# GRU scan on TensorE: r's state product of the row scans as two products, with v and with u

## The reference

```python
seq = xs.reshape(b * A, T, c) @ Wi.T + bi            # 192 -> 64
x_gates = seq @ W_ih.T + b_ih
def step(h, xg):
    hg = h @ W_hh.T + b_hh
    xr, xz, xn = split(xg); hr, hz, hn = split(hg)
    r = sigmoid(xr + hr)
    z = sigmoid(xz + hz)
    n = tanh(xn + r * hn)
    h_new = (1.0 - z) * n + z * h
out = hs @ Wo.T + bo
x = x + (right + down + left + up) / 4.0
```

## Time and profile before

| | |
|---|---|
| median of three runs | 2478.38 us |
| profiled execution | 2490.38 us |
| its span, first to last instruction | 2488.6 us |
| TensorE clock granted, mean | 0.985 of full speed |
| busy: PE matmul, PEld weight load | 2186.1 us (88%), 1416.7 us (57%) |
| busy: DVE, ACT, POOL | 2014.4 (81%), 1579.7 (63%), 1532.9 us (62%) |

### The profile page before, as it was taken

One profiled execution on the slowest core, in us unless ns is written; L12 is line 12 of the kernel. 1 busy time (PEld: TensorE's weight loads), 2 busy tenths in 40 slices (PEclk: granted clock), 3 DMA queues, 4 the chain that ended last, 5 costly groups with the idle time before them and its releaser, 6 DMA issues.

```text
span 2488.6 us, 79958 instructions
## 1 busy us (share of the span) xinstructions
PE 2186.1 (88%) x31528; PEld 1416.7 (57%) x31528; DVE 2014.4 (81%) x4982; ACT 1579.7 (63%) x3401; POOL 1532.9 (62%) x2114
## 2 busy tenths in 40 slices
PE   0579999899979999898979999899989999999995
PEld 0345555566646666565646666565656666555574
DVE  7309999877769999887869999887867888888874
ACT  0126666677758788676758888676757888666600
POOL 2007777667767677666767777666766777777600
PEclk9999999999999999999999999999999999999998
DMA  9993332256789997589999998589986665334699
GB/s 347 275 239 102 97 98 76 75 148 207 240 230 249 238 256 202 150 226 258 313 272 245 250 254 211 144 224 263 316 261 172 154 151 128 74 95 95 166 326 359
DMA packets 325716, 509.19 MB, mean 205 GB/s; under 512 B 24928, under 2 KB 140000, under 8 KB 325344
## 3 DMA queue, kind: packets, MB, share of 16 engines
q1 hardware_dynamic: 307296, 478.23, 70.1%
q10 hardware_dynamic: 18048, 25.85, 3.0%
HBM read 352.98 MB, written 151.01 MB: 203 GB/s over the span
## 4 chain that ended last, share of the span: by engine, by line
DVE 34%; PE 30%; ACT 17%; issue 8%; DMA 6%; POOL 3%; SPq 1%; ACTq 0%; DVEq 0%; POOLq 0%
PE bank L855 18%; DVE r L989 12%; DVE r L994 11%; ACT r L655 7%; DMA work<-x 5%; DVE h L1008 5%; ACT z L659 4%; ACT bank L663 3%; DVE bank L999 3%; PE bank L835 3%; PE bank L953 2%; ACT work L650 2%; PE bank L837 2%; DVE bn L981 1%; PE bank L856 1%
## 5 line engine op out<-in xcount | busy, mean ns | idle before, releaser
L855 PE MATMUL bank<-h,wh 64*64 64x256 f32 x6144 | 1498.8, 386 | 112.6 <-DVE h L1008 97.2
L835 PE MATMUL bank<-seq,wx 64*64 64x256 f32 x6144 | 1549.3, 385 | 43.6 <-DMA seq<-seq_next 21.6
L837 PE MATMUL bank<-seq,wx 64*64 64x256 f32 x6144 | 1549.9, 385 | 0.7 <-issue 0.7
L856 PE MATMUL bank<-h,wh 64*64 64x256 f32 x6144 | 1500.5, 387 | 0.2 <-issue 0.2
L537 POOL TENSOR_TENSOR v<-z,h 128x256 f32<-128x256 f32 x1024 | 747.0, 730 | 719.4 <-ACT z L659 693.2
L855 PEld LDWEIGHTS bank<-h,wh 64*64 64x64 f32 x6144 | 712.7, 133 | 577.4 <-DVE h L1008 409.2
L835 PEld LDWEIGHTS bank<-seq,wx 64*64 64x64 f32 x6144 | 755.2, 133 | 223.5 <-DVE r L994 119.1
L545 POOL TENSOR_TENSOR hsum<-hsum,h 128x256 f32<-128x256 f32 x1024 | 751.7, 734 | 117.7 <-DVE h L1008 98.4
L837 PEld LDWEIGHTS bank<-seq,wx 64*64 64x64 f32 x6144 | 752.7, 133 | 33.1 <-issue 4.2
L989 DVE SCALAR_TENSOR_TENSOR r<-bank,bhh,r 128x256 f32<-128x256 f32 x1024 | 490.0, 479 | 277.2 <-ACT r L655 236.5
L856 PEld LDWEIGHTS bank<-h,wh 64*64 64x64 f32 x6144 | 702.6, 133 | 0.8
(11 more groups left out here) (95 smaller groups left out, 2443.6 us busy)
## 6 DMA issues: line engine op xcount, KB each, us to landing
work<-x SPq DMA_DIRECT2D x384, 384.0 KB, 6.4
out<-work SPq DMA_DIRECT2D x192, 384.0 KB, 4.7
work<-x SPq DMA_DIRECT2D x143, 512.0 KB, 7.1
work<-x SPq DMA_DIRECT2D x286, 128.0 KB, 7.4
work<-x SPq DMA_DIRECT2D x32, 768.0 KB, 6.8
seq_next<-work SPq DMA_DIRECT2D x48, 512.0 KB, 6.7
work<-hsum_last SPq DMA_DIRECT2D x48, 512.0 KB, 7.5
seq<-x SPq DMA_DIRECT2D x17, 512.0 KB, 7.2
```

Source lines behind the costliest of these rows:

```text
L835: pe.matmul(as_pair(ps[LOW, :], c), wx[HIGH, gate, :], px[HIGH], start=start, stop=False, skip_group_check=True)
L837: return pe.matmul(as_pair(ps[HIGH, :], c), wx[LOW, gate, :], px[LOW], start=start, stop=False, skip_group_check=True)
L855: pe.matmul(ps[LOW, 0:N2], wh[LOW, gate, :], state[LOW], start=start, stop=True, skip_group_check=True)
L856: return pe.matmul(ps[HIGH, 0:N2], wh[HIGH, gate, :], state[HIGH], start=start, stop=True, skip_group_check=True)
```

## The change

In all steps but the first of a scan, r's state part of the rows is no longer one product with h, but two: v_r multiplies v by the weights of r, and u_r multiplies u by the same weights with the sign turned (wr_minus, made once by VectorE). Both add to the bank that holds x_r. v_r stands on TensorE at the end of the step before, behind x_z of the rows (and behind the unit halves or the projection that go beside the input's products); u_r stands where h_r stood, and waits for u and not for h. The wait for h moves to h_n. u of the rows is now a tensor in SBUF, u0; u of the columns stays in its bank, and the columns' r is as it was.

```diff
+        wr_minus = sb("wr_minus", [P, D])
+        u0 = sb("u0", [P, N2])
...
+        u_of = [u0[:, :], hn_ps[1][:, N2:2 * N2]]
...
+            def product(w, rhs):
+
+                pe.matmul(rx_ps[0][LOW, 0:N2], w[LOW], rhs[LOW], start=False, stop=True, skip_group_check=True)
+                return pe.matmul(rx_ps[0][HIGH, 0:N2], w[HIGH], rhs[HIGH], start=False, stop=True, skip_group_check=True)
+
+            def v_r(g, t):
+
+                pe.wait_ge(v_ready[0], T * g + t)
+                pe.wait_ge(x_rn_ready[0], T * g + t + 1)
+                product(wh[:, 0, :], v[:, 0, :])
+
+            def u_r(g, t):
+                pe.wait_ge(u_ready[0], T * g + t)
+                product(wr_minus[:, :], u0[:, :]).then_inc(pre_r[0], 1)
...
             def h_n(g, t, c):
+                if c == 0 and t > 0:
+                    pe.wait_ge(h_ready[0], state_before(g, t))
                 h_part(hn_ps[c], 2, t, c, True).then_inc(pre_n[c], 1)
...
-                    h_r(g, t, 0)
+                    if t == 0:
+                        h_r(g, t, 0)
+                    else:
+                        u_r(g, t)
...
                     if beside_input:
                         unit_half(g, u, 1)
+                    if t + 1 < T:
+                        v_r(g, t + 1)
                     if u is not None and not beside_input:
...
+                dve.tensor_scalar(wr_minus[:, :], wh[:, 0, :], -1.0, None, ALU.mult).then_inc(w_ready, 1)
...
-                dve.scalar_tensor_tensor(out=hn_ps[c][:, N2:2 * N2], in0=z[:, c, :], scalar=1.0, in1=hn_ps[c][:, 0:N2],
+                dve.scalar_tensor_tensor(out=u_of[c], in0=z[:, c, :], scalar=1.0, in1=hn_ps[c][:, 0:N2],
                                          op0=ALU.subtract, op1=ALU.mult).then_inc(u_ready[c], 1)
...
-                dve.tensor_tensor(h[:, c, t % 2, :], v[:, c, :], hn_ps[c][:, N2:2 * N2], ALU.subtract)\
+                dve.tensor_tensor(h[:, c, t % 2, :], v[:, c, :], u_of[c], ALU.subtract)\
```

More of the change, by code:

```diff
@@ L960, in _ @@
             mean_bias(0)
-            pe.wait_ge(w_ready, 4)
+            pe.wait_ge(w_ready, 5)
             project_first()
```

## The result

The changed kernel takes 2535.28 us (median of four runs, 2529.05 to 2536.51) against 2479.41 (2475.55 to 2480.62) for the kernel before: a ratio of 1.0216 [1.0191, 1.0241], 56 us slower. The forecast was 2528 with a range of 2465 to 2600. The profiled execution took 2529.05 us, 38.7 more than before's; that is less than the medians say mostly because in before's profile the first scan began 9.8 us later (at 184.2 against 174.4); from 60 to 120 us its loads moved 281 GB/s against 301.

A forecast was written before the change was run, and what follows sets the result against it. The prediction took a loop of short dependent steps through VectorE, TensorE and ScalarE, no single engine, to bound the kernel. Terms 29 + 7 + 14 = +50 us on the 2478.4 us median gave 2528 us, range 2465 to 2600.

The forecast's parts named there:

- The hold in the first scan: First scan's statistics stage: rows' h, with two SBUF inputs, waits for GpSimd's v; +0.45 x 64 steps = +29 us.
- Not held in the other first halves: First halves of scans two to four: h starts no later than v, cost 0; other ends 58 us and 29 us.
- The later halves: Later halves of the scans, 228 steps: h waits for v, partly repaid by an earlier t1; +0.06 each, +14 us.
- The quick t1: Later halves: rows' t1 follows h's end by about 0.80 us, where it came 1.26 behind before.
- TensorE's product at no cost outside 16 crowded steps: Added product on TensorE hidden, except where a unit half follows because a projection shares the step: 16 x 0.45 = 7 us.
- the earlier r: Rows' r not waiting for h: up to 0.10 a step where VectorE is full; 15 us possible in later halves, unsummed.
- Held in all stages (1): Rival, chance 0.20: h waits for v in all stages with statistics or units; up to 58 + 29, about 2600 us.
- Faster (2): Rival, chance 0.14: h doesn't wait for v at full size, or starts no later than v; 2464 us.
- Cancel (3): Rival, chance 0.08: h waits in the first stage (+29 + 7), later halves gain 36 us; 2478 us.
- TensorE the bound (4): Rival, chance 0.04: the added product on TensorE isn't hidden; 508 x 0.45 = 229 us, so 2707 us.
- The rule from the Trainium skill: VectorE with two SBUF inputs and GpSimd reading SBUF exclude each other entirely; first scan's stage loses 9 us more.

## Why the prediction was right

**The hold in the first scan.** Forecast: h ends 0.27 behind v, the step is 4.45 to 4.55, +29 us. Measured: 0.28, 4.47 (mean of the half 4.46), +25.7. h lasts 0.88, a little less than the 0.9 to 1.0 that I gave, as it starts 0.13 behind v and no longer 0.09. The loop's parts held too: t1 follows the rows' h 1.17 after its end (1.26 before), the lower of the two values that I gave. Small operations of 128x3 beside GpSimd were enough to size it.

**Not held in the other first halves.** As forecast, for 176 of 180 steps: h starts at most 0.01 behind v there. The one row that I went by stood 0.04 ahead; the median of the second scan is 0.00 already in the kernel before, so there the margin was thinner than I took it to be, and luck is in it. The term was 0 and the stretch lost 3.0, but not evenly: -4.6 in the second scan, +4.6 and +3.0 in the third and fourth (mean steps of 4.03, 4.15 and 4.12, for the 4.05 that I gave). The kernel in which v waits for t2 and nothing is held loses no less there (793.6 - 787.4 = 6.2), so this isn't the hold.

**The later halves.** Forecast +14 for a hold in each step and +7 for the added product: 21. Measured +26.1. The sum was close by luck, the parts weren't. h is held in half of the steps, not in all, and a held one costs more than the 0.06 that I gave. Which are held goes with the schedule: in steps 72 to 125 of the first three scans h is held in each of the 69 in which a projection only ends, and in 11 of the 93 in which one begins; the last scan has no projection, and there 22 of 54 are held, as in the rows at 2292 to 2301 (4.34 and 3.92, mean 4.13). Against the kernel in which v waits for t2, the hold is worth 1116.1 - 1097.7 = 18.4, some 0.18 for each of the 102 held steps. The other 7.7 can't be put down to anything: the two controls with the wait and without the added product lie as far above before in these halves (6.9 and 9.6) with medians that can't be told from before's. The quick t1 (0.8 behind h's end) was right for the later half of the first scan alone, 0.83 in 28 of its 29 held steps. In the other scans the columns' h and the units' addition on VectorE come between, and it is 1.1 in most, as from 2293.54 (2292.61 + 0.93) to 2294.65 in the rows above.

**TensorE's product at no cost outside 16 crowded steps.** Mis-sized: alone it costs 18 us (12 to 24 by its interval), not 7. The crowded steps are 10 in each of the two scans and not 8, but that makes only 9 us of the 7. It didn't show in the total because the gain that I had left out of the sum where h isn't held, the earlier r, pays for it, which is luck: with all products and next to no hold, the kernel is 3 us from the one before (interval -1 to +6). So 18 - 15 = 3 stands where I had 7 and no gain; the 15 is by difference, from two kernels with the same number of products, and as loose as the 18.

**The rivals.** Held in all stages (1): refuted by the second to fourth first halves. Its time was also added up wrongly: 58 + 29 is 87, and 2528 + 87 = 2615 lies outside the range, where I wrote 72 and 2600. Faster (2): h is not early by itself; once the wait puts it ahead, the step of the first scan is 3.99, so the point from which that rival decides was rightly put, but the whole is then level and not 14 us faster. Cancel (3): its gain and loss do cancel, but only without the hold. TensorE the bound (4): 18 in place of 229, even though the chain of waits shows 82% TensorE in the kernel with the added product alone.

**The rule from the Trainium skill** (SBUF — State Buffer, "Who interferes with whom") that the two exclude each other for the whole instruction, whoever came first, asked for 9 us more in the first scan, by h at v's end + 0.41. The rows say 0.28. In the other half of the rule, which no row of before showed, the traces do agree: a v that comes second is held for h. There is less of that than of a whole instruction in the recorded times as well: v ends 0.59 behind h's end, for a duration of 0.73. Either way the second operation ends 0.13 or 0.14 sooner than its own recorded duration behind the first.

## What to carry to other kernels

An operand moved from PSUM to SBUF can bring a VectorE operation with two inputs into conflict with GpSimd, and whether that costs is judged from the two start times in the trace, in each stage by itself and over many steps: a few hundredths decide which of the two is held, and here the kernel before had them almost as the changed kernel has. Where the one on the path comes second, it can help to let the other wait for the instruction just ahead of it on its engine, not for its own end. A term put at "hidden" deserves a run of its own, since here a cost of 18 us and a gain of 15 hid each other.

## What was not expected of the hardware

- How sharply the start parts the two cases, though not by itself. Over all 512 steps of the changed kernel, h goes first in each that starts up to 0.03 us behind v (v is then stretched: 0.88 us where h is 0.12 ahead, 1.01 at the same time, 1.03 at 0.03 behind), and is held in each that starts 0.06 to 0.48 behind. In the kernel with u in SBUF alone much the same values part them: up to 0.03 not held, from 0.06 on held. But in the kernel with h ahead of the columns' t2 the three h at 0.03 are held, so where it turns depends on more than the recorded starts, and what that is is open.
- An h with an input in PSUM isn't touched, in the same program: in the kernel with the split only in the holes, 82 steps whose h reads PSUM start 0.07 or 0.08 behind v, and in all of them h takes 0.41 and v 0.72 or 0.73.
- The loss can come in every step or in every other one. In the first scan's first half, where VectorE is full, it comes in all. In the last scan's later half, where VectorE has slack, it alternates in the rows at 2292 to 2301, but in the kernel with u in SBUF alone it comes there in all 54 steps too, at 4.55 us each; so slack alone doesn't end it. Why the held state settles or alternates was argued from the loop of the forecast and not tried by itself; nor was a kernel tried that makes the columns' v on another engine.
